# A 7x7 dilated convolution with pixels on the partitions, in a kernel of convolution, token choice and attention

## What is computed

```python
y = conv(x, conv_w, 7x7, dilation 5, padding 15)      # 32 channels -> 1
imp = sigmoid(gelu(bn(y)))                            # importance of a pixel
_, idx = top_k(imp.reshape(B, -1), 192); idx = sort(idx)
tokens = (x * imp)[idx] + pos[idx]                    # 192 tokens of an image
t1 = layernorm(tokens + attention(tokens))            # 8 heads of 4
t2 = layernorm(t1 + relu(t1 @ w1.T + b1) @ w2.T + b2)
xf = x * imp;  xf[idx] = t2;  out = x + xf
```

## Time and profile before

| | us |
|---|---|
| median of 3 runs | 1157.81 |
| lowest, highest | 1154.83, 1164.65 |
| profiled execution, own time | 1156.72 |
| its span, first to last instruction | 1154.8 |

### The profile page before, as it was taken

One profiled execution on the slowest core, in us unless ns is written; L12 is line 12 of the kernel. 1 busy time (PEld: TensorE's weight loads), 2 busy tenths in 40 slices (PEclk: granted clock), 3 DMA queues, 4 the chain that ended last, 5 costly groups with the idle time before them and its releaser, 6 DMA issues.

```text
span 1154.8 us, 21628 instructions
## 1 busy us (share of the span) xinstructions
PE 944.7 (82%) x6440; PEld 743.1 (64%) x6440; DVE 841.7 (73%) x2114; ACT 769.4 (67%) x1899; POOL 636.3 (55%) x853
## 2 busy tenths in 40 slices
PE   3887977599968997999899989898787688389676
PEld 2665655377747875787687868785665477277544
DVE  5345779478858986898789988896697589466654
ACT  2445654287747895888678877886588487178443
POOL 5332234832676468647774687458545764772542
PEclk9898989799989998999899999999899599689755
DMA  9998978575655999899898989876565466448778
GB/s 244 280 293 235 279 210 236 144 190 157 167 149 157 264 260 247 230 261 279 239 263 249 262 265 264 249 211 161 152 182 146 121 175 184 121 118 237 204 237 264
DMA packets 176677, 247.90 MB, mean 215 GB/s; under 512 B 65937, under 2 KB 72433, under 8 KB 176561
## 3 DMA queue, kind: packets, MB, share of 16 engines
q1 hardware_dynamic: 168368, 244.11, 75.3%
q0 software_dynamic: 8192, 2.40, 1.4%
HBM read 124.59 MB, written 121.83 MB: 213 GB/s over the span
## 4 chain that ended last, share of the span: by engine, by line
PE 41%; DVE 19%; POOL 10%; ACT 10%; DMA 9%; issue 9%; SPq 1%; ACTq 0%; POOLq 0%; DVEq 0%
PE cv L524 12%; PE sc L643 7%; PE xb L508 5%; PE pp L656 4%; PE tr L558 4%; DMA table<-xt 3%; POOL tok_imp L1006 3%; POOL tok_x L1006 3%; PE ib L571 3%; DVE res L1347 2%; POOL tok_pos L1006 2%; PE ms L672 2%; DMA X<-in_x 2%; ACT wgt L840 2%; ACT pr L869 2%
## 5 line engine op out<-in xcount | busy, mean ns | idle before, releaser
L524 PE MATMUL cv<-X,w_conv 128*128 128x330 f32 (+1 forms) x1024 | 302.4, 422 | 27.7 <-POOL X L980 25.7
L524 PEld LDWEIGHTS cv<-X,w_conv 128*128 128x128 f32 x1024 | 191.1, 201 | 63.7 <-issue 26.1
L840 ACT ACTIVATE wgt<-ib,eps_col,mom 128x440 f32<-128x440 f32 (+1 forms) x256 | 178.0, 702 | 41.0 <-DVE res L1347 27.5
L1142 DVE TENSOR_SCALAR_CACHE_REDUCE junk<-flat,th 128x385 bf16<-128x385 f32 x200 | 122.2, 611 | 105.6 <-ACT th L826 104.6
L508 PE MATMUL xb<-cst,X 128*110 128x128 f32 x900 | 151.0, 294 | 39.6 <-ACT xt L806 23.6
L1043 POOL TENSOR_SCALAR res<-res,mom 128x440 f32<-128x440 f32 (+1 forms) x152 | 96.4, 638 | 150.8 <-DVE res L1347 149.3
L643 PE MATMUL sc<-k_b,qm 128*128 128x192 f32 x768 | 166.2, 343 | 14.4 <-DVE pixf L1242 7.4
L806 ACT COPY xt<-xb 110x512 f32<-110x512 f32 x225 | 131.7, 585 | 47.8 <-PE xb L508 34.9
L869 ACT ACTIVATE pr<-sc,least 128x192 f32<-128x192 f32 x384 | 137.3, 416 | 16.0 <-DVE least L1311 14.9
L1347 DVE SCALAR_TENSOR_TENSOR res<-tr,mom,wgt 128x440 f32<-128x440 f32 (+1 forms) x192 | 122.0, 641 | 33.8 <-PE tr L558 26.0
L1123 DVE BATCH_NORM_STATS2 stats<-X 128x6 f32<-128x458 f32 (+3 forms) x256 | 139.5, 574 | 6.8 <-DMA X<-in_x 6.8
(11 more groups left out here) (172 smaller groups left out, 1533.5 us busy)
## 6 DMA issues: line engine op xcount, KB each, us to landing
table<-xt SPq DMA_DIRECT2D x240, 224.0 KB
rt<-table SPq DMA_DIRECT2D x240, 224.0 KB, 3.9
out<-res SPq DMA_DIRECT2D x320, 137.5 KB
X<-in_x SPq DMA_DIRECT2D x64, 412.5 KB, 5.1
X<-in_x SPq DMA_DIRECT2D x64, 343.8 KB, 5.6
conv_rows<-cvr SPq DMA_DIRECT2D x64, 188.0 KB
y<-conv_rows SPq DMA_DIRECT2D x64, 165.4 KB
out<-res SPq DMA_DIRECT2D x64, 68.8 KB
```

Source lines behind the costliest of these rows:

```text
L524: last = mm(cv[:, 0:CUT[half]], w_conv[:, 4 * q + z], X[:, m % XI, at0:at0 + CUT[half]], start=z == 0, stop=z == 3)
L840: last = A(wgt[:, n % 2, at0:at0 + w], ib[:, at0:at0 + w], ACT.Identity, scale=mom[:, NB * g + b, 2:3], bias=eps_col[:, 1:2])
L1142: v.tensor_scalar(junk[:, 0:FL], flat[:], th[:, 0:1], None, ALU.is_ge, ALU.add, accum_out=cnt[:]).then_inc(cnt_ok, 1)
```

## The change

The convolution is turned round: for each of 5 residues r of the row and 6 blocks of rows (`KG`), the stationary operand is 110 pixels of X (128 x 110) and the moving one is 35 to 70 columns of weights, so that output pixels j lie on partitions and (row, tap) in the columns (`conv_rows`). ACT copies three and then two residues to `taps` (`rows_copy`), and seven matmuls with shifted identity (`shift`) add the taps up in PSUM (`conv_taps`), which ACT copies to `yy`. The store to `conv_rows`, the read back and the sum of DVE are gone. The steps stand in other slots: see the constants. `norm_first` is in three slots; `project` in two; the split of the importance to POOL has its own tile `im` and stands one slot later. The one who adds the mean is set by the string `MEAN_ON`, by slot mod 30 (P 14, A 7, D 9), for all groups.

```diff
-        LOAD, INTO, MOMENTS, NORMAL = -21, -11, -5, (-2, -1, -1)
-        TAPS, SUM = (10, 17, 25, 31), (15, 20, 28, 32)
-        GELU, IMP_OUT, FLAT, SEARCH, IMP_IN = 33, 35, 38, 40, 58
-        MASKS, SCANS, RANKS, HOT, PICK, INDEX = 65, 66, 68, 70, 72, 72
-        GATHER, GATHERS = 74, (3, 3, 3, 3, 3, 3, 3, 3)
-        REST, SPLIT, PARTS_OUT = 74, (83, 84, 85), 87
-        EMBED, PROJECT, SCORES = 82, 86, 87
-        MIX, NORM, FEED, NORM2 = 114, 115, 118, 120
-        SCATTER, BACK, IMPB = 122, 127, (123, 127, 135, 142)
+        LOAD, INTO, MOMENTS, NORMAL = -20, -11, -5, (-2, -1, -1)
+        TAPS = 5
+        GELU, IMP_OUT, FLAT, SEARCH, IMP_IN = 29, 31, 35, 36, 54
+        MASKS, SCANS, RANKS, HOT, PICK, INDEX = 61, 62, 64, 66, 68, 68
+        GATHER, GATHERS = 70, (3, 3, 3, 3, 3, 3, 3, 3)
+        REST, SPLIT, PARTS_OUT = 74, (84, 85, 86), 88
+        EMBED, PROJECT, SCORES = 77, 81, 83
+        MIX, NORM, FEED, NORM2 = 109, 110, 114, 116
+        SCATTER, BACK, IMPB = 120, 125, (121, 125, 133, 140)
+        MEAN_ON = "PPAPPAPPPDPDDPADDADAPDPAPPDDAP"
...
+        rows_at = {BASE[b] + r: (b, r) for b in range(NB) for r in range(DIL)}
+        taps_at = {BASE[b] + TAPS: b for b in range(NB)}
...
-        in_dmas = [(BACK + 1 + u - GATHER) % U < len(GATHERS) or (BACK + 1 + u - SCATTER) % U < 4 for u in range(U)]
-        adder = [[(DVE_ADDS if g >= G - 3 else ACT_ADDS) if in_dmas[u] else POOL_ADDS for u in range(U)] for g in range(G)]
+        adder = [[(POOL_ADDS, ACT_ADDS, DVE_ADDS)["PAD".index(MEAN_ON[(BACK + 1 + u) % U])] for u in range(U)] for g in range(G)]
...
-            def round_out(g, r):
-                b, q = r // 4, r // 2 % 2
-                sp.wait_ge(cv_cp, upto(cv_cp, g, r))
-                if g:
-                    sp.wait_ge(y7_in[b], upto(y7_in[b], g - 1))
-                sp.dma_start(conv_rows[2 * b + q, 0:KS * OUT_T * CW].rearrange("(p x) -> p x", x=CW), cvr[:, q, :]
-                             ).then_inc(cv_w[q], 16)
-            def taps_in(g, b):
-                for q in range(2):
-                    sp.wait_ge(cv_w[q], upto(cv_w[q], g, b))
-                if g:
-                    sp.wait_ge(y_ok, upto(y_ok, g - 1, b))
-                else:
-                    sp.wait_ge(pad_w, upto(pad_w, 0))
-                for q in range(2):
-                    taps = conv_rows[2 * b + q].rearrange("(k x) -> k x", k=KS)[:, 0:55 * (H + 15)]
-                    sp.dma_start(y7[55 * q:55 * q + 55, b], taps.rearrange("k (p r) -> p k r", r=H + 15)[:, :, 0:H]
-                                 ).then_inc(y7_in[b], 16)
...
-            def conv_part(g, r, first, last_z):
-                b, q, half = r // 4, r // 2 % 2, r % 2
+            def conv_rows(g, b, r):
                 m = NB * g + b
-                if first == 0:
-                    if r:
-                        pe.wait_ge(cv_cp, upto(cv_cp, g, r - 1))
-                    elif g:
-                        pe.wait_ge(cv_cp, upto(cv_cp, g - 1))
-                for z in range(first, last_z):
-                    blk_in = 2 * q + z
-                    pe.wait_ge(xn_ok, upto(xn_ok, g, 3 * b + blk_in // 2))
-                    at0 = BW * blk_in + CUT[0] * half
-                    last = mm(cv[:, 0:CUT[half]], w_conv[:, 4 * q + z],
-                              X[:, m % XI, at0:at0 + CUT[half]], start=z == 0, stop=z == 3)
-                if last_z == 4:
+                if r == 0 and m:
+                    pe.wait_ge(y_cp, upto(y_cp, 0, m - 1))
+                if r == SPLIT_R:
+                    pe.wait_ge(cv_cp, upto(cv_cp, g, 2 * b))
+                at0 = WIDE * (r % SPLIT_R)
+                for k in range(KG):
+                    pe.wait_ge(xn_ok, upto(xn_ok, g, 3 * b + k // 2))
+                    low = 4 * k - KS // 2
+                    lo, hi = max(0, low), min(H // DIL, low + KS + 3)
+                    w0 = KS * (KS + 3) if k == KG - 1 else KS * (lo - low)
+                    row = H * (DIL * k + r)
+                    last = mm(cv[0:H, at0 + KS * lo:at0 + KS * hi], X[:, m % XI, row:row + H], w_conv[:, w0:w0 + KS * (hi - lo)],
+                              start=k == 0, stop=k == KG - 1, skip_group_check=True)
+                if r in (SPLIT_R - 1, DIL - 1):
                     last.then_inc(conv_ok, 1)
+            def conv_taps(g, b):
+                pe.wait_ge(cv_cp, upto(cv_cp, g, 2 * b + 1))
+                for k in range(KS):
+                    last = mm(cv[0:H, 0:H], taps[:, k], shift[:, DIL * k:DIL * k + H], start=k == 0, stop=k == KS - 1)
+                last.then_inc(y_ok, 1)
...
-            def project(g):
-                pe.wait_ge(tokt_cp, upto(tokt_cp, g))
-                for p in range(2):
-                    for sem, value in sc_read[p][-1:]:
-                        pe.wait_ge(sem, value)
-                    sc_read[p].append((qk_cp, upto(qk_cp, g, p)))
+            def project(g, p):
+                if p == 0:
+                    pe.wait_ge(tokt_cp, upto(tokt_cp, g))
+                for sem, value in sc_read[p][-1:]:
+                    pe.wait_ge(sem, value)
+                sc_read[p].append((qk_cp, upto(qk_cp, g, p)))
+                last = mm(sc[:, p, 0:K], (wq, wk)[p][:], tok_t[:], start=True, stop=True)
+                if p == 0:
+                    last.then_inc(qkv_ok, 1)
+                    return
                 for sem, value in ms_read[-1:]:
                     pe.wait_ge(sem, value)
                 ms_read.append((v_cp, upto(v_cp, g)))
...
-                ms_read.append((v1_ok, upto(v1_ok, g)))
+                ms_read.append((y1_rd, upto(y1_rd, g)))
...
-                    for part in rounds[n][0:1]:
-                        conv_part(g, part[0], part[1], part[2])
+                    if n in rows_at:
+                        conv_rows(g, *rows_at[n])
+                    if n in taps_at:
+                        conv_taps(g, taps_at[n])
...
-            def round_copy(g, r):
-                b, q, half = r // 4, r // 2 % 2, r % 2
-                act.wait_ge(conv_ok, upto(conv_ok, g, r))
-                if half == 0 and (g or b):
-                    act.wait_ge(cv_w[q], upto(cv_w[q], 0, NB * g + b - 1))
-                rows = cvr[:, q, :].rearrange("p (r j) -> p r j", j=H + 15)[:, 3 * half:5 if half else 3, 15:H + 15]
-                nc.scalar.copy(rows, cv[0:KS * OUT_T, 0:CUT[half]].rearrange("p (r j) -> p r j", j=H)).then_inc(cv_cp, 1)
+            def rows_copy(g, b, part):
+                act.wait_ge(conv_ok, upto(conv_ok, g, 2 * b + part))
+                lo, hi = ((0, SPLIT_R), (SPLIT_R, DIL))[part]
+                nc.scalar.copy(taps[:].rearrange("p k (q r) -> p r q k", r=DIL)[:, lo:hi],
+                               cv[0:H, 0:WIDE * (hi - lo)].rearrange("p (r q k) -> p r q k", r=hi - lo, k=KS)).then_inc(cv_cp, 1)
+            def taps_copy(g, b):
+                act.wait_ge(y_ok, upto(y_ok, g, b))
+                if g:
+                    act.wait_ge(imp_ok, upto(imp_ok, g - 1))
+                nc.scalar.copy(yy[:, b], cv[0:H, 0:H]).then_inc(y_cp, 1)
...
-            for w in (imp_b, y7, ge, parts, zrow, k_b):
+            for w in (imp_b, ge, parts, zrow, k_b):
...
-                for g, n in at(s, NORM + 1):
+                for g, n in at(s, NORM + 3):
...
-            def importance_sum(g, b):
-                dve.wait_ge(y7_in[b], upto(y7_in[b], g))
-                v.reduce_sum(yy[:, b], y7[:, b].rearrange("p k j -> p j k"), AX).then_inc(y_ok, 1)
...
-            def norm_first(y, bias, res_in, out_v):
-                for half in range(2):
-                    post(v.tensor_tensor(out_v[:, halves[half]], y[:, halves[half]], rep[:, bias], ALU.add))
-                sync()
-                link(v.tensor_tensor(out_v[:], out_v[:], res_in[:], ALU.add))
+            def norm_in(g, y, bias, res_in, out_v, read):
+                post(v.tensor_tensor(out_v[:, halves[0]], y[:, halves[0]], rep[:, bias], ALU.add))
+                v.tensor_tensor(out_v[:, halves[1]], y[:, halves[1]], rep[:, bias], ALU.add).then_inc(read, 1)
+                dve.wait_ge(read, upto(read, g))
+                sync()
+                post(v.tensor_tensor(out_v[:], out_v[:], res_in[:], ALU.add))
+            def norm_mean(out_v):
+                sync()
                 link(v.reduce_sum(rs[:, 0, :], out_v[:], AX))
                 link(v.tensor_scalar(rs[:, 0, :], rs[:, 0, :], 1.0 / C, None, ALU.mult))
-                link(v.tensor_tensor(out_v[:], out_v[:], rs[:, 0, :].unsqueeze(2).to_broadcast([HALF, 8, C]), ALU.subtract))
+                post(v.tensor_tensor(out_v[:], out_v[:], rs[:, 0, :].unsqueeze(2).to_broadcast([HALF, 8, C]), ALU.subtract))
+            def norm_var(out_v):
+                sync()
                 link(v.tensor_tensor(sq[:], out_v[:], out_v[:], ALU.mult))
                 link(v.reduce_sum(rs[:, 3, :], sq[:], AX))
                 return v.tensor_scalar(rs[:, 1, :], rs[:, 3, :], 1.0 / C, EPS, ALU.mult, ALU.add)
...
```

(26 more changed lines are left out.)

118 lines of the change are left out of this document (51 added, 67 removed).

## The result

The changed kernel takes 1186.74 us (median of 4 runs, 1178.26 to 1191.34) against 1156.87 for the kernel before in the same comparison (4 runs, 1154.83 to 1164.65): a ratio of 1.023, with a 95% interval of 1.020 to 1.027. It is slower by 30 us where 33 less were forecast, and outside the range. The profiled execution is the slowest of the four, 1191.34 us.

A forecast was written before the change was run, and what follows sets the result against it. No engine was taken as full: transfers bound the fill, and a chain of POOL's serial gathers, then DVE and PE, the full period. Terms -3 -18 +20 -7 +15 -35 -11 +4 sum to -35: 1124 us median, range 1088 to 1180.

The forecast's parts named there:

- Term 1: Convolution matmuls on PE: 74 records an image at 97 ns each, 7.2 us in place of 7.4; -3 us.
- Term 2: Transfers and fill: conv stores, reads and their chain gone, first two groups' stretches shorter; -18 us, bounds -5 and -30.
- Term 7: New wait: first conv row of an image needs all three of POOL's normalisation parts; +4 us, bounds 0 and +20.
- Term 6: DVE, ACT and POOL work: sums gone, more finishes on DVE (+16 of work), fewer copies on ACT; -11 us.
- Terms 3 and 4: Gathers: longer piece +20 us, shorter landing -7; slots: six more outside the gathers, +15.
- Term 5: Norms and projection: norms cut into three slots shorten the chain, PE's wait through bank `ms` named; -35 us, bounds 0 and -45.
- loads exposed at 201 ns: Bound on the convolution's matmuls: each load exposed at its recorded 201 ns, 14.9 us an image, +239 over 32 images.
- (a): Rival: gathers decide, norm cut gains nothing, landings stay; about 1180, between 1169 and 1202 us; chance 0.14.
- (b): Rival: matmul loads exposed at 201 ns each, half on the chain; about 1240, above 1202 us; chance 0.06.
- (c): Rival: nothing gained, gathers and slots (+28) eat a half-size norm gain and a fill of 10; 1146 to 1169 us; chance 0.20.
- (d): Rival: transfers bound the full period too, 25 us more gain; about 1098, between 1080 and 1105 us; chance 0.14.
- the mark of (a): Sign for (a): a full period above 120 us with DVE's wait for the gathers above 60 us in all.

The follow-up runs named there:

- e15: Kernel before with the new convolution alone, 110 moving columns in each conv matmul and the copy to taps walked in the other order; 1151.5 us, ratio 0.996.
- e14: e12 with each norm in one slot again; 1156.6 us, ratio 0.999.
- e12: e7 with the old finish rule (POOL 18 of 30 slots, otherwise ACT, or DVE in the last three groups) in place of the string; 1142.2 us, ratio 0.987.
- e7: e4 with ACT's copy to taps walked in the other order, reading with a stride and writing short runs, same result; 1154.5 us, ratio 0.996.
- e4: Changed kernel with 110 moving columns in every conv matmul, the added ones zeros, same result; 1158.6 us, ratio 0.999.
- e5: Kernel before with the new convolution alone, in the old slots, with 110 moving columns in each conv matmul; 1165.0 us, ratio 1.006.
- e6: Changed kernel with 90 moving columns in every conv matmul, the added ones zeros; 1160.9 us, ratio 1.002.
- e10: Changed kernel with 80 moving columns in every conv matmul, the added ones zeros; 1161.3 us, ratio 1.004.
- e13: Changed kernel with the old finish rule in place of the string; 1176.2 us, ratio 1.016.
- e11: e7 with each norm in one slot again, POOL's half in the next; 1171.4 us, ratio 1.012.
- e3: Changed kernel with ACT's copy to taps made plain, without its stride, so that taps are mixed up; 1176.7 us, ratio 1.015.

## Why the forecast was wrong, step by step

The runs give a ladder from the kernel before to the changed one, by medians, beside the terms of the forecast:

| step | measured, us | forecast |
|---|---|---|
| new convolution at 110 columns, copy turned: before to e15 | -5 | terms 1, 2, 7, sums and copies of 6: -31 |
| slots, gathers, projection: e15 to e14 | +5 | terms 3 and 4: +28 |
| norms cut: e14 to e12 | -14 | term 5: -35 |
| string: e12 to e7 | +12 | in term 6: +4 |
| copy as written: e7 to e4 | +4 | in term 6, a bound: +5 |
| few columns, clock: e4 to changed | +28 | none |

By the comparisons' intervals each of these is known to 3 to 7 us, so the rungs of 4 and 5 us are hardly clear of nothing. The forecast missed by 63 us, of which by the rungs about 28 are the clock, 26 the first rung and 21 the norms, with 12 for string and copy, and the slots, 23 us cheaper than priced, hid part of it.

**Term 1, right in its price at one clock, wrong in carrying it to the other; this is the step that failed.** The 97 ns a record were borrowed from rows at a high clock. At that clock the new matmuls take 91 ns (12 in 1.09 us), even less. The Trainium skill ("TensorE: Matmul & The Clock Gate", "LDWEIGHTS (loading the stationary operand)") gives a load its columns divided by 1.2, by which 92 ns is the estimate for 110; at the high clock the trace's spacing agrees, at the low one it is 176 ns. With 110 columns the chain of e12 has

```profile
108.73 1.17 PE cv L488 x12
```

97 ns a record. But a price in ns from one stretch was carried into another as if the clock were given. At the low clock the record takes 176 ns. The price in ns rested on the unspoken assumption that a new kind of work leaves the clock alone; the earlier trace rows has a clock column, and the forecast made no term of it. The bound "loads exposed at 201 ns" was nearer in the low stretch than the value taken, for another reason than the one it was given for. (The prediction sets the -10 of that estimate against -7; the term itself has -3 on the chain.) The same page of the Trainium skill says, in "What's actually happening", that "activity releases the throttle". By PE's busy share the trace doesn't agree: in the changed kernel it is busy 13.0 us of the first 31 at a clock of 1.00, 87.8 of 100 at 0.65, and 41.0 of the last 59 at 0.50. That more streamed columns bring the clock back is shown (e4, e5, e6, e10); through what quantity is not.

**Term 2, right in size in the fill, given back later.** The bytes went as forecast, 247.9 to 224.5 MB, 23.4 less. In e15, at nearly the clock of before, the first conv matmuls of groups 0 and 2 lie 110 us apart, against 121 before, and the index of the first group is ready at 178 us against 192. That is most of the 18. By the index of the last group nothing is left, 967.6 against 967.9 us. The three full periods between stand at 121.8, 119.5 and 119.5 us, against 121.1, 119.2 and 119.4 before. The time is lost at the two ends: the steps from the first index to that of group 2 last 107.5 and 115.8 us against 103.7 and 112.0, those from group 5 to group 7 last 111.0 and 94.7 against 107.5 and 93.1. At the front end e15 has a clock of 0.87 from 200 to 300 us where 0.90 stood; what made the late steps longer wasn't taken apart. So the fill gave back what it had gained before the last group came. In the changed kernel the fill was not even shorter, 61 us from group 0's first conv matmul to group 1's in place of 57: from 31 to 90 us the clock is 0.88 and the DMA share 0.81. The chain of that stretch is 56% PE, with single steps of 2.11 us as at the low clock, and 29% loads of X, so transfers alone no longer bound it.

**Terms 3 and 4, mechanism right, cost too large.** The gathers take 34.6 us in a full period, and 34.3 were forecast. From the index to the embedding of groups 0 to 5 are 38 to 40 us in the changed kernel, 37 to 38 in e12 and 34 to 38 before. But the period doesn't grow with it. In e13 the full periods are 121.7, 119.3 and 119.3 us with gathers of 33.5 us, the same as before and as e15 with 31.1. Nor does the embedding simply follow the gathers: in e15 it comes 39 to 41 us behind the index, later than in e12, though the gathers are shorter. So the gather piece wasn't a serial part of the period in the sense that the sum took: 2.4 us more inside it came off elsewhere. The shorter landing doesn't show either: from the last gather of group 3 to its embedding are 4.2 us, 4.1 before. What does set 119.3 us in three kernels so unlike in PE's and DVE's work, no run here tells.

**Term 5, right in sign, twice too large, and not by the wait that it named.** PE's wait of 16.1 us for the norm's end is gone, as forecast. But this wait doesn't need the cut. In e15, with each norm whole and the bank released at its end, 4.1 us of it are left (there PE multiplies queries and keys ahead of the wait, so this part of term 5 stands in the ladder's first rung); in e11 and e14, with each norm whole and the bank released after its first two additions, none. The cut brings a wait of its own that the sum left out, PE for POOL's `ra`: 0.3 us in e14, 16.1 in e12 and 15.1 in the changed kernel. The cut still gains 14 to 17 us, in place of 35. With it POOL's wait for the norm's end falls (32.6 us in e14, 13.5 in e12); whether that is what the gain consists of no run shows.

**Term 6, two sizes off.** The stride made the copy 839 ns, against the 480 of a plain one. It was given as a bound of +5 on the chain, and cost 4 or 5 at 110 columns, 10 at the low clock and 13 in the old slots. The finishes on DVE were sized by the mean of the earlier trace rows, 438 ns, and that is right for nearly all of them; but four take 3.2 us each in their new slots, so that the whole is 26 us more in place of 16. The string cost 8 to 12 us where a quarter of 16 was taken. The sum also took the 20 us that POOL loses as worth nothing, which fits: POOL waits longer.

**Term 7, small as forecast.** PE's waits for POOL's parts are 25.0 us as before (25.7), in more and shorter pieces. In the old slots (e15) they are 43.2 us, so the new slots give something back here.

**The rivals.** (a) ended in the right region, near 1180, by a mechanism that didn't happen: its term 5 of nothing is refuted by e11 and e14, and its gather piece by e13. (b), loads exposed at full clock, is refuted by 91 ns. (c) has the time of the schedule at the high clock, 1158.6 in e4, but by the wrong terms. (d), transfers as the bound of the full period, is refuted by e15: 2.8 MB less a group, and the same period. Of the marks set for the changed kernel, those of the gathers' length, the projection's wait and the DMA share (0.83) came out; the conv work near 230 us, the fill under 50 us and the period of 117 us didn't, and DVE waited for the gathers in 3 places only, not in nearly all groups. The period is above 120 us, but DVE's wait for the gathers is 29.5 us and not above 60, so the mark of (a) isn't met either. The mark "conv and taps together near 230 us on PE" was a poor one: it set a sum of chain prices against busy time, in which matmuls overlap. The old convolution has 7.4 x 32 = 237 us by price and 302.4 busy, and in e4, at a clock like that of before, the new one has 275.6.

## What to carry to other kernels

A price in ns for a TensorE instruction holds only at the clock it was read at: where a change turns few long matmuls into many short ones behind loads as wide as these, give the clock a rival of its own, and price it from rows at both levels. When the clock of a stretch falls while PE is busy, try wider moving operands before blaming the schedule: here zero columns bought 28 us. When the mean of an operation differs between two kernels, ask for its median and its longest: here 4 of 72 made nearly the whole difference. And separate the parts of a large change: this one held a gain of 1.3% beneath three losses (columns, string, copy).

## What the runs showed of the hardware

- A busy PE at a low clock: busy 87.8 of 100 us, clock 0.65, with matmuls of 35 to 70 moving columns behind loads of 110. With 70 columns it was 0.70, with 80, 90 and 110 in the same places 0.87, 0.88 and 0.88.
- Where these loads set the pace the level costs nearly its ratio: 12 records in 2.11 us at the one and 1.09 us at the other, 1.94 times.
- A copy on ACT from PSUM to SBUF, 110 partitions by 462 floats: 542 ns where both sides run plainly (e3), 556 where it is read with a stride in PSUM and written in runs of three floats (e7), 971 where it is read in order and each next element is written 440 bytes on (the changed kernel). With 308 floats, and runs of two, the three are 417, 512 and 707 ns. The Trainium skill ("SBUF — State Buffer", "Specifications (TRN2)") speaks of a penalty for each access that crosses to a new 16-byte line; the order of the three fits, though no run here isolates the line.

```profile
L788 ACT COPY taps<-cv 110x462 f32<-110x462 f32 x32 | 17.4, 542 | 17.9 <-PE cv L486 17.6
...
L789 ACT COPY taps<-cv 110x462 f32<-110x462 f32 x32 | 17.8, 556 | 11.5 <-PE cv L487 11.4
...
L788 ACT COPY taps<-cv 110x462 f32<-110x462 f32 x32 | 31.1, 971 | 18.8 <-PE cv L486 18.5
```

- The same DVE operation on `res`, 128 x 440, has a median of 439 to 441 ns under both finish rules. Four times it took 3.22 us, each time from 0.5 us before POOL's last two parts of a normalisation to 0.2 us behind them (e7; the same four in the changed kernel). What holds it was not taken apart.
